# Another plan for one instruction stream: hand-over times, the pace of the attention heads, and transposes issued before their buffer is free

## The reference

```
diff = a1 - lam * a2
out  = einsum('bhts,bhsd->bhtd', diff, v)
out  = (out - mean) * rsqrt(var + EPS) * gn_w + gn_b      # statistics over a head's 64 channels
x    = layernorm(x + (out * 0.2) @ Wo)
```

```
hidden = silu(x @ wu.T) * (x @ wg.T)
x      = layernorm(x + hidden @ wd.T)
```

## Time and profile before

| | |
|---|---|
| median of 3 runs | 2279.82 us |
| profiled execution: time / span | 2284.03 / 2282.2 us |
| PE busy | 2197.1 us, 96% |
| DVE busy | 1713.9 us, 75% |
| ACT busy | 1464.8 us, 64% |
| POOL busy | 1192.8 us, 52% |
| mean granted PE clock | 0.993 |

### The profile page before, as it was taken

How to read it: one execution, slowest core, us unless ns; L and a number is a source line. 1 busy time by engine, 2 the same in 40 slices (tenths; PEclk the granted TensorE clock), 3 DMA queues, 4 the chain that set the end, 5 groups by cost and what they waited for, 6 DMA issues and landing times.

```text
span 2282.2 us, 41409 instructions
## 1 busy us (share of the span) xinstructions
PE 2197.1 (96%) x13602; PEld 1395.9 (61%) x13602; DVE 1713.9 (75%) x3829; ACT 1464.8 (64%) x3362; POOL 1192.8 (52%) x1919
## 2 busy tenths in 40 slices
PE   8999999898999999999999999999999999999998
PEld 5566665656666666666667666666666666544443
DVE  4787988898888888878877888888877888532343
ACT  1787776767677767767667776777766777421232
POOL 0565757675644655556654565565545455421232
PEclk9999999999999999999999999999999999999999
DMA  6868565756441223233443232252243111202000
GB/s 221 245 197 236 170 184 181 231 175 204 139 125 47 79 90 96 89 93 106 146 147 102 61 102 79 62 170 75 65 130 107 44 55 34 74 18 76 1 19 19
DMA packets 258003, 256.53 MB, mean 112 GB/s; under 512 B 31360, under 2 KB 199424, under 8 KB 255744
## 3 DMA queue, kind: packets, MB, share of 16 engines
q1 hardware_dynamic: 246016, 220.26, 32.0%
q10 hardware_dynamic: 11776, 33.63, 4.6%
HBM read 182.53 MB, written 71.30 MB: 111 GB/s over the span
## 4 chain that ended last, share of the span: by engine, by line
PE 72%; DVE 12%; issue 5%; POOL 5%; DMA 3%; ACT 2%; SPq 1%; DVEq 0%; POOLq 0%; ACTq 0%
PE F L1085 17%; PE S L1007 10%; PE F L1026 9%; PE F L1094 9%; PE F L1052 8%; PE F L1072 8%; PE F L987 7%; DVE e_long L1349 4%; DVE e_long L1420 2%; DMA dq<-hl 2%; POOL linv L1276 2%; PE F L1060 1%; POOL coef L1277 1%; DVE e_short L1420 1%; DVE e_short L1349 1%
## 5 line engine op out<-in xcount | busy, mean ns | idle before, releaser
L1276 POOL TENSOR_TENSOR linv<-lsum,powers 128x2 f32<-128x2 f32 x512 | 411.6, 804 | 425.9 <-ACT e_long L1146 344.9
L1146 ACT ACTIVATE e_long<-e_long,nmax 128x768 f32<-128x768 f32 (+3 forms) x512 | 505.6, 989 | 131.8 <-DVE nmax L1349 129.5
L1349 DVE CUSTOM_DVE_ANT_0 e_long<-S,mask_b 128x768 f32<-128x768 f32 (+3 forms) x512 | 516.6, 1020 | 87.2 <-PE S L1007 76.1
L1007 PE MATMUL S<-kstk,qstk 128*128 128x384 f32 (+5 forms) x1536 | 520.2, 425 | 34.7 <-DVE nmax L1349 28.9
L1007 PEld LDWEIGHTS S<-kstk,qstk 128*128 128x128 f32 x1536 | 268.8, 190 | 203.4 <-issue 90.9
L1136 ACT ACTIVATE dt_long<-F 128x512 f32<-128x512 f32 (+3 forms) x544 | 259.9, 516 | 152.3 <-PE F L987 149.0
L1420 DVE SCALAR_TENSOR_TENSOR e_long<-e_long,coef 128x1024 f32<-128x1024 f32 (+3 forms) x256 | 276.9, 1082 | 49.8 <-POOL coef L1277 48.8
L1052 PE MATMUL F<-xT,wr 128*128 128x512 f32 x640 | 306.3, 607 | 3.8 <-issue 1.6
L1146 ACT ACTIVATE e_short<-e_short,nmax 128x384 f32<-128x384 f32 (+3 forms) x512 | 284.1, 559 | 40.2 <-DVE nmax L1349 38.7
L1289 POOL TENSOR_TENSOR hid<-th,hid 128x512 f16<-128x512 f32 x128 | 148.4, 1161 | 278.8 <-ACT hid L1189 171.4
L1349 DVE CUSTOM_DVE_ANT_0 e_short<-S,mask_b 128x384 f32<-128x384 f32 (+3 forms) x512 | 241.1, 487 | 46.4 <-PE S L1007 35.2
(11 more groups left out here) (111 smaller groups left out, 3301.8 us busy)
## 6 DMA issues: line engine op xcount, KB each, us to landing
qstk<-dq SPq DMA_DIRECT2D x512, 128.0 KB, 2.8
dq<-hl SPq DMA_DIRECT2D x32, 1024.0 KB, 5.2
wr<-in_w_proj ACTq DMA_DIRECT2D x48, 512.0 KB, 4.1
kstk<-dk SPq DMA_DIRECT2D x64, 256.0 KB, 4.9
da<-ra SPq DMA_DIRECT2D x32, 512.0 KB, 3.4
at_sb<-da SPq DMA_DIRECT2D x32, 512.0 KB, 4.3
dk<-hl SPq DMA_DIRECT2D x8, 1024.0 KB, 5.4
wt<-in_w_up SPq DMA_DIRECT2D x16, 512.0 KB, 5.6
```

What stands on the lines that cost most here:

```text
L1007: last = nc.tensor.matmul(slot[:, h, :], qstk[:, duo % 4, 2 * r + m, :].bitcast(F32R), kstk[:, g % 2, m, h * w:(h + 1) * w].bitcast(F32R), ...
L1146: nc.scalar.activation(e, e, ACT.Exp, bias=nmax[:, u % 8:u % 8 + 1], scale=-1.0, accum_out=lsum[:, n % 4, m:m + 1]).then_inc(s_exp, 1)
L1276: link(nc.gpsimd.tensor_tensor(linv[:, a % 8, :], lsum[:, a % 4, :], mone, ALU.pow))
L1349: nc.vector.tensor_tensor_reduce(out, slot, mask, -1.0, -NEG, ALU.add, ALU.min, nmax[:, u % 8:u % 8 + 1]).then_inc(s_negmax, 1)
```

## The change

Four edits in the planner. No function of the kernel that issues instructions is touched, so the multiset of instructions is the same and only their order, the bank of some uses and the semaphore values that follow from both move.

```
-HAND_OVER = {"pe": .3, "act": .4, "dve": .3, "pool": .3}
+HAND_OVER = {"pe": .4, "act": .4, "dve": .4, "pool": .4}
...
-PACE = 3.75
+PACE = 3.8
...
-STUCK = 0
+STUCK = 2
...
                 if item.what == "scores" and item.a and item.b == 0:
-                    if item.a >= 128:
-                        r = max(r, end[ITEM("scores", item.a - 16)] + PACE * 16)
+                    r = max(r, end[ITEM("scores")] + PACE * item.a)
```

## The result

The changed kernel takes 2318.67 us (median of four runs, 2313.62 to 2326.01), the kernel before beside it 2280.9 us. The ratio is 1.0166, with a 95% interval of 1.0135 to 1.0197: slower by 37.8 us. The forecast was 2298 us, so the direction was right and the time lies in the range, but the growth is about twice the 18.5 us forecast.

What follows compares the result with a forecast made beforehand. PE was taken to bound all but the first quarter. Tail +65.6, heads 128 to 511 -47.1, first quarter 0 and stuck turns 0 gave +18.5 us on the median 2279.8: 2298 us, 8 in 10 from 2268 to 2342.

Steps and rivals of the forecast that it cites:

- the mean hold: Stuck turns: each holds its bank about 2 us longer, a small part of all bank time; priced 0, -7 to 28 us.
- the tail: Behind the last score map: 304 more matmuls on a PE without idle to hide them, +65.6 us.
- what the other stage gives back: Heads 128 to 511: less PE work but 3.3% idle, so 1377.9 us, 47.1 us less.

Runs made afterwards that it cites:

- e10_pace385: The kernel before with PACE 3.85 where 3.75 stood; 2292.16 us, ratio 1.0056.
- e11_pace400: The kernel before with PACE 4.0 where 3.75 stood; 2309.19 us, ratio 1.0128.
- e1_hand: The kernel before with only the hand-overs of 0.4 from the change; 2292.48 us, ratio 1.0048.
- e3_stuck: The kernel before with only STUCK = 2 from the change; 2336.36 us, ratio 1.0238.
- e5_no_stuck: The whole change but with STUCK = 0, so no stuck turns; 2285.82 us, ratio 1.0033 against the kernel before.

## What to carry over

When an order of work is fixed, price an early grab of a shared buffer by the worst place, not by the mean hold: list who holds the other buffers at that moment, and follow the release of each; a holder whose release lies behind the waiting instruction turns a slow neighbour into a stop of the engine that feeds the others. Work moved into a stage that one engine fills can be priced to a few us from the order and one row, as the tail was here; what the other stage gives back can't, as e10_pace385 and e11_pace400 show. And before a difference of half a per cent between two planned orders is put down to an edit, re-plan with a meaningless change: here that alone cost 9 to 12 us.

## What the runs showed of the hardware

- Around a stop of 10 us (276 to 286 us) the granted clock was 0.92 in the window of 20 us in which it began and 0.74 in the one in which it ended, as shown above; before, a wait of 3.7 us left 0.91.
- Busy time of PE isn't a constant of the program. In the 17 orders profiled at mean clocks of 0.986 to 0.996, the same 13602 matmuls were busy 2190.0 us (e1_hand) to 2220.2 us (e3_stuck). The clock doesn't explain it: e5_no_stuck has 2192.4 us at 0.986 and e3_stuck 2220.2 us at 0.987. So a comparison by idle time alone misses up to 30 us.
